# Loads of the next stage issued in the last turn of the stage before, and channel mixing's first keys taken chunk by chunk

## The reference

```python
# time mixing (RWKV): mixes, projections, a scan over the 128 rows, group norm, gate
x = x + att * g @ Wo.T
# channel mixing
xn2 = _ln(x, ln2_w, ln2_b)
sx2 = _token_shift(xn2, state[:, i0])     # row t-1 minus row t
xk = xn2 + sx2 * ffn_maa_k
xr = xn2 + sx2 * ffn_maa_r
rr = jax.nn.sigmoid(xr @ ffn_Wr.T)
kk = jnp.square(jax.nn.relu(xk @ ffn_Wk.T))
x = x + rr * (kk @ ffn_Wv.T)
# twice cross attention with 16 heads of 128 on keys and values of ctx, then an MLP 512 -> 2048 -> 512 with gelu
x = x + cross_attention(layer_norm(x), ctx, ...)
x = x + cross_attention(layer_norm(x), ctx, ...)
x = x + gelu(layer_norm(x) @ w_fc1 + b_fc1) @ w_fc2 + b_fc2
```

## Time and profile before

| | before |
|---|---|
| median of 3 runs | 3049.38 us (3048.84 to 3049.61) |
| the profiled execution, its own time | 3048.88 us |
| its span, first to last instruction | 3047.1 us |
| mean granted clock of TensorE | 0.975 of full speed |
| busy: PE, DVE, ACT, POOL | 94%, 58%, 38%, 18% |

### The profile page before, as it was taken

One profiled execution on the slowest core, in us unless ns is written; L12 is line 12 of the kernel. 1 busy time (PEld: TensorE's weight loads), 2 busy tenths in 40 slices (PEclk: granted clock), 3 DMA queues, 4 the chain that ended last, 5 costly groups with the idle time before them and its releaser, 6 DMA issues.

```text
span 3047.1 us, 40885 instructions
## 1 busy us (share of the span) xinstructions
PE 2878.6 (94%) x14864; PEld 2177.5 (71%) x14864; DVE 1776.0 (58%) x2615; ACT 1162.6 (38%) x2537; POOL 536.5 (18%) x375
## 2 busy tenths in 40 slices
PE   5989898985979999999999999999999999999899
PEld 2333333333768888888888878788888888888787
DVE  5989889895755444455444464454444554444644
ACT  3232323232434343445334343344334444433432
POOL 2857667571001000000000010010000000000100
PEclk8999899997999999999999999999999999999999
DMA  5010010102223111111111112121111111111011
GB/s 160 1 29 28 23 34 2 41 1 99 73 101 133 38 37 49 38 56 39 47 43 35 55 35 62 44 88 38 55 38 39 48 39 55 38 50 32 23 54 55
DMA packets 54780, 148.72 MB, mean 49 GB/s; under 512 B 6256, under 2 KB 7536, under 8 KB 53584
## 3 DMA queue, kind: packets, MB, share of 16 engines
q1 hardware_dynamic: 51824, 143.80, 14.2%
q0 software_dynamic: 2880, 3.94, 0.6%
HBM read 131.20 MB, written 12.58 MB: 47 GB/s over the span
## 4 chain that ended last, share of the span: by engine, by line
PE 67%; DVE 2%; ACT 1%; issue 0%; DMA 0%; ACTq 0%; DVEq 0%
PE ca_ps L60 19%; PE ca_ps L62 19%; PE ca_ps L61 19%; PE ca_ps L1967 4%; PE ca_ps L1951 4%; PE ca_ps L1959 2%; PE ca_ps L1993 1%; DVE ca_stats L68 0%; DVE ca_xres L1728 0%; DMA ca_xres<-in_ctxT 0%; DVE ca_wq_lo L1686 0%; ACT ca_sk L1644 0%; DVE ca_ctx_lo L1759 0%; DVE ca_h_lo L1753 0%; ACT L1644 0%
## 5 line engine op out<-in xcount | busy, mean ns | idle before, releaser
L1728 DVE TENSOR_TENSOR ca_xres<-ca_xres,ca_ps 128x512 f32<-128x512 f32 x384 | 263.9, 687 | 244.1 <-PE ca_ps L62 239.1
L1515 ACT ACTIVATE ca_pr<-ca_ps,ca_nb 128x129 f32<-128x129 f32 x512 | 181.4, 368 | 511.3 <-DVE ca_nb L1711 511.2
L60 PE MATMUL ca_ps<-ca_h_hi,ca_wq_hi 128*128 128x512 f32 x768 | 313.2, 408 | 3.8 <-DVE ca_h_lo L1753 3.3
L613 DVE TENSOR_TENSOR_SCAN tm_xn<-tm_wd,tm_vb 128x512 f32<-128x512 f32 x256 | 298.5, 1208 | 12.7
L62 PE MATMUL ca_ps<-ca_h_hi,ca_wq_lo 128*128 128x512 f32 x768 | 303.0, 394 | 0.0
L61 PE MATMUL ca_ps<-ca_h_lo,ca_wq_hi 128*128 128x512 f32 x768 | 301.0, 392 | 0.0
L60 PE MATMUL ca_ps<-ca_wv_hi,ca_ctx_hi 128*128 128x256 f32 x1024 | 297.9, 291 | 0.0
L62 PE MATMUL ca_ps<-ca_wv_hi,ca_ctx_lo 128*128 128x256 f32 x1024 | 287.4, 281 | 0.0
L61 PE MATMUL ca_ps<-ca_wv_lo,ca_ctx_hi 128*128 128x256 f32 x1024 | 287.2, 280 | 0.0
L1468 POOL TENSOR_TENSOR ca_dv<-ca_bvr 128x256 f32<-128x256 f32 x32 | 24.7, 772 | 1453.7 <-DVE ca_v L1696 1443.7
L60 PE MATMUL ca_ps<-ca_wo_hi,ca_ct_hi 128*128 128x512 f32 x640 | 253.5, 396 | 0.2 <-DVE ca_xres L1728 0.2
(11 more groups left out here) (232 smaller groups left out, 5788.4 us busy)
## 6 DMA issues: line engine op xcount, KB each, us to landing
ca_sq<-in_wq SPq DMA_DIRECT2D x49, 512.0 KB, 5.2
ca_so<-in_wo SPq DMA_DIRECT2D x48, 512.0 KB, 3.5
ca_sk<-in_wk SPq DMA_DIRECT2D x33, 512.0 KB, 6.4
ca_sv<-in_wv SPq DMA_DIRECT2D x32, 512.0 KB, 3.6
ca_bvr<-in_bvb SPq DMA_DIRECT2D x32, 256.0 KB, 3.9
tm_xq<-in_x SPq DMA_DIRECT2D x16, 256.0 KB, 3.8
tm_xres<-in_x SPq DMA_DIRECT2D x4, 1024.0 KB, 5.1
x_dram<-tm_xres SPq DMA_DIRECT2D x4, 1024.0 KB, 4.3
```

Source lines behind the costliest of these rows:

```text
L60: pe.matmul(out, lhs[0], rhs[0], start=first, stop=False)
L613: v.tensor_tensor_scan(state[t % 2][:, d, :], wd[:, g].rearrange("p b t -> p (b t)"), pair[:, d, :], 0.0, ALU.mult, ALU.add).then_inc(scan ...
L1515: ins = act.activation(pr[hd][:, b, :], ps[:, BANK_SC + b // 2, o:o + KW], ACT.Exp, bias=nbs[hd][:, b:b + 1], scale=SCALE, accum_out=sms[h ...
L1728: v.tensor_tensor(xres[U.h][:, U.quad * 4 + b, :], xres[U.h][:, U.quad * 4 + b, :], ps[:, BANK_O + b % 2, :], ALU.add).then_inc(o_out, 1)
```

## The change

Loads that a stage began with are issued by the preceding stage. `xq`, `xres`, `eps`, the constants and a tensor `raw` of 12 x 512 columns now belong to all stages; time mixing's weights `wv`, `wk`, `wr` are the three parts of `raw`, and so are channel mixing's `gate`, `relu`, `gy`. In the last turn of time mixing SP issues channel mixing's five first loads, each weight when its third of `raw` has been read for the last time, and then the last store. In the last turn of channel mixing it issues six loads of cross attention ahead of the last store. The wait for the last store moves from the end of a block into the next one: in channel mixing to the head of SP's stream, in cross attention behind the first load of `x3`. On DVE and PE channel mixing's first keys are written chunk by chunk. In `first()` ACT's `key_out(C, 0)` goes ahead of `roots(0)`.

```diff
 # time_mix, SP
+            def store(q):
+                sp.wait_ge(res_added, q * 4 + 4)
+                sp.dma_start(x2[bass.ds(q * 4, 4)].rearrange("b t e -> t b e"), xres[:]).then_inc(x2_out, 16)
...
-                sp.wait_ge(res_added, q * 4 + 4)
-                sp.dma_start(x2[bass.ds(q * 4, 4)].rearrange("b t e -> t b e"), xres[:]).then_inc(x2_out, 16)
-            sp.wait_ge(x2_out, NQ * 16 + 16)
+                    store(q)
+            sp.wait_ge(xn0_ready, NQ * 4)
+            sp.dma_start(xq[:], x2[0:4].rearrange("b t e -> t b e")).then_inc(cm_first_in, 16)
+            sp.dma_start(common["prev0"][:], io["prev0"]).then_inc(cm_first_in, 16)
+            for w, (full, count) in enumerate(((v_full, NQ * 4), (k_full, NQ * 4), (r_full, NQ * 4))):
+                sp.wait_ge(full, count)
+                sp.dma_start((wv, wk, wr)[w], io["l0w"][5 + w]).then_inc(cm_first_in, 16)
+            store(NQ - 1)
 # channel_mix, SP
-            sp.dma_start(xq[:], x2[0:4].rearrange("b t e -> t b e")).then_inc(x_in, 16)
-            for tile, name in ((vec, "vec"), (ident, "ident"), (prev, "prev0")):
-                sp.dma_start(tile[:], io[name]).then_inc(const_in, 16)
-            for j in range(3):
-                sp.dma_start(raw[j][:], io["l0w"][5 + j]).then_inc(w_in[j], 16)
+            sp.wait_ge(x2_out, NQ * 16 + 16)
...
                 sp.dma_start(xres[:], x2[bass.ds(q * 4, 4)].rearrange("b t e -> t b e")).then_inc(res_in, 16)
+                if not more:
+                    sp.dma_start(early["ctx"][:, 0:4, :], io["ctxT"][:, :, 0:QT]).then_inc(early["c_in"][0], 16)
+                    sp.dma_start(early["ctx"][:, 4:8, :], io["ctxT"][:, :, QT:2 * QT]).then_inc(early["c_in"][1], 16)
+                    sp.dma_start(early["sk"][:], io["wk"][0]).then_inc(early["wk_in"], 16)
+                    sp.dma_start(early["sv"][:], io["wv"][0]).then_inc(early["wv_in"], 16)
+                    sp.dma_start(early["hv"][:], io["head_vec"]).then_inc(early["const_in"], 16)
+                    sp.dma_start(early["bvr"][:], io["bvb"][0]).then_inc(early["dv_in"], 16)
                 sp.wait_ge(added, q * 4 + 4)
...
-            sp.wait_ge(x3_out, NQ * 16 + 16)
 # channel_mix, DVE
+            def first_mix():
+                v.tensor_copy(xn[:, :, :, 0], prev[:, :, 0:4]).then_inc(prev_ready, 1)
+                v.wait_ge(prev_ready, 1)
+                for c in range(EC + 1):
+                    if c < EC:
+                        v.wait_ge(xn_ready, c + 1)
+                        v.tensor_tensor(sx[:, c, :] ...
+                        v.wait_ge(sx_ready, c + 1)
+                        v.scalar_tensor_tensor(out=xf[0][:, c, :] ...
+                    if c > 0:
+                        v.wait_ge(hi_ready, c)
+                        v.tensor_tensor(x_lo[0][:, c - 1, :], xf[0][:, c - 1, :], x_hi[0][:, c - 1, :], ALU.subtract).then_inc(split_ready, 1)
 # channel_mix, PE
-            keys(0)
+            for c in range(EC):
+                pe.wait_ge(split_ready, c + 1)
+                for f in range(EC):
+                    ins = mm3(pe, mm[:, f, :], (w_hi[:, 0, c, f * P:(f + 1) * P], w_lo[:, 0, c, f * P:(f + 1) * P]),
+                              (x_hi[0][:, c, :], x_lo[0][:, c, :]), c == 0, c == EC - 1)
+                    if c == EC - 1:
+                        ins.then_inc(k_full, 1)
 # cross_attend, ACT, first()
-                act.wait_ge(const_in, 48)
-                act.wait_ge(ready, 1)
+                act.wait_ge(const_in, 16)
+                key_out(C, 0)
                 roots(0)
-                key_out(C, 0)
                 key_out(C, 1)
```

More of the change, by code:

```diff
@@ L103, in sem @@
             return ctx.enter_context(nc.semaphore("tm_" + n))
-        vec = sb("vec", [P, NV])
-        ident = sb("ident", [P, P])
+        vec, ident, eps, xq, xres, raw = [common[n] for n in ("vec", "ident", "eps", "xq", "xres", "raw")]
+        wv, wk, wr = [raw[:, j * EC:(j + 1) * EC, :] for j in range(3)]
         head_sum_u = sb("head_sum_u", [P, EC, P])
@@ L1007, in _, with channel_mix @@
             closing(NQ - 1)
-def channel_mix(nc, io, x2, x3):
+def channel_mix(nc, io, x2, x3, common, early):
     with ExitStack() as ctx:
@@ L1018, in sem @@
             return ctx.enter_context(nc.semaphore("cm_" + n))
[L1020 to L1023, removed]
+        vec, ident, eps, prev, xq, xres = [common[n] for n in ("vec", "ident", "eps", "prev0", "xq", "xres")]
+        gate, relu, gy = [common["raw"][:, j * EC:(j + 1) * EC, :] for j in range(3)]
         rest = sb("rest", [1, 1])
@@ L1152, in link, with norm @@
                 return step
-            def norm(q):
-                v.wait_ge(x_in, q * 16 + 16)
+            def norm(q, first=False):
+                if first:
+                    v.wait_ge(first_in, N_FIRST)
+                else:
+                    v.wait_ge(x_in, q * 16)
                 layernorm_dve(v, xq, lnx, stats, mv, std, rstd, bn_done, stats_ready, std_ready, xn0_ready, q, link(q))
@@ L1264, in _, with cross_attend @@
             values(NQ - 1)
-def cross_attend(nc, io, x3, out):
+def cross_attend(nc, io, x3, out, common, early):
     HT = 8
@@ L1291, in cross_attend @@
         h2 = two("h", [P, EC, HT * L])
-        xres = [sb("xres%d" % h, [P, HT, E]) for h in range(2)]
-        lt = sb("lt", [P, 4, E])
+        xres = [common["raw"][:, 0:HT, :], early["ctx"]]
+        lt = common["raw"][:, HT:HT + 4, :]
         stats = sb("stats", [P, 4, 6])
@@ L1461, in _ @@
         def _(gp):
-            gp.memset(eps[:], EPS).then_inc(ready, 1)
             def value_bias(i):
@@ L2110, in build, with sb, sem @@
     x2 = nc.dram_tensor("x2_dram", (B, L, E), F32, kind="Internal").ap()
-    time_mix(nc, io, x2)
     x3 = nc.dram_tensor("x3_dram", (B, L, E), F32, kind="Internal").ap()
-    channel_mix(nc, io, x2, x3)
-    cross_attend(nc, io, x3, out)
+    with ExitStack() as whole:
+        def sb(n, s, d=F32):
+            return whole.enter_context(nc.sbuf_tensor(n, s, d))
+        def sem(n):
+            return whole.enter_context(nc.semaphore(n))
+        common = {"vec": sb("vec", [P, NV]), "ident": sb("ident", [P, P]), "eps": sb("eps", [P, 1]),
+                  "prev0": sb("prev0", [P, EC, B]), "xq": sb("xq", [P, 4, E]), "xres": sb("xres", [P, 4, E]),
+                  "raw": sb("raw", [P, 3 * EC, E]), "cm_first_in": sem("cm_first_in"),
+                  "x2_out": sem("x2_out"), "x3_out": sem("x3_out")}
+        time_mix(nc, io, x2, common)
+        early = {"hv": sb("ca_hv", [P, 11 * NH]), "ctx": sb("ca_xres1", [P, 8, E]), "sk": sb("ca_sk", [P, EC, 256]),
+                 "sv": sb("ca_sv", [P, EC, 256]), "bvr": sb("ca_bvr", [P, 2, 256]),
+                 "c_in": [sem("c_in%d" % quad) for quad in range(2)],
+                 "wk_in": sem("wk_in"), "wv_in": sem("wv_in"), "dv_in": sem("dv_in"), "const_in": sem("const_in")}
+        channel_mix(nc, io, x2, x3, common, early)
+        cross_attend(nc, io, x3, out, common, early)
 def vec_table(a):
```

75 lines of the change are left out of this document (30 added, 45 removed).

## The result

| | before | changed |
|---|---|---|
| median | 3049.11 us of 4 runs (3048.76 to 3049.61) | 3026.31 us of 4 runs (3024.28 to 3033.33) |
| the profiled execution, its own time | 3048.88 us | 3033.33 us |
| its span | 3047.1 us | 3031.4 us |
| mean granted clock | 0.975 | 0.977 |

The ratio is 0.9927 (95% interval 0.9913 to 0.9941), 22.8 us by the medians; I had said 21.1 and 3028.3. Note that the profiled execution of the changed kernel is the slowest of its four, 7 us above the median. The explanation has to account for that too.

What follows compares the result with a forecast made beforehand. PE, busy 94% of the span, was taken as the bound, with its longest stalls at the two seams. Terms 3.9 + 8.0 − 0.9 + 3.9 + 5.8 + 0.4 = 21.1 us off gave 3028.3 us, range 3024.0 to 3033.0.

Steps and rivals of the forecast that it cites:

- Store waits, 3.9 + 3.9: End of time mixing and of channel mixing: moving the last store's wait behind the barrier takes 3.9 us off each.
- The rival that a block end holds the engines: Both block ends wait for outstanding DMAs anyway, so the 3.9 us stay: gain 13.3, time 3036; chance 0.07.
- First seam, 8.0: Time mixing to channel mixing: early loads bring the first `xn` 8.05 instead of 16.07 us after the barrier, 8.0 off.
- Chunked keys, 0.9 lost: Channel mixing's first turns: keys end 2.5 us earlier, but idle PE and a fallen clock make it net 0.9 lost.
- PE, being late, would wait less in the next turn: Channel mixing's second turn: PE, slowed in the values, waits less and may keep its clock, giving 1.0 us back.
- Rule on the clock: Second transposes of channel mixing: about 3.5 us of idle PE drops the clock, so they take 3.65 us, not 1.97.
- Second seam, 5.8: Channel mixing to cross attention: early loads start PE 5.62 instead of 11.46 us after the barrier, 5.8 off.
- `first()`, 0.4 gained: Cross attention's first unit: with `key_out(C, 0)` ahead of the roots, the first query comes 0.4 us earlier after PE's start.
- A second slip: Second seam: the forecast had the rows of `x3` land 5.8 us after their request, as `xq` did.
- The rest, no change: From cross attention's first query to the end, the time should be that of before.

Runs made afterwards that it cites:

- e2: Changed kernel with the waits for the last stores put back at the end of both blocks, loads still early: 3034.11 us, ratio 0.9947.
- e3: Changed kernel's tensor placing only; loads late, store waits at block ends, keys and roots order as before: 3053.77 us, ratio 1.0011 to the kernel before.
- e1: Changed kernel with channel mixing's first keys and first mix as before, without chunks: 3023.60 us, ratio 0.9913.
- e11: The changed kernel itself, unaltered, timed again in the last group: 3024.50 us, ratio 0.9924.
- e0: The changed kernel itself, unaltered, timed again in the second group: 3027.51 us, ratio 0.9936.
- e7: Changed kernel with the second half of ctx rounded and split earlier in `first()`: 3024.82 us, ratio 0.9921.
- e8: Changed kernel with the roots ahead of the first `key_out` again, as in the kernel before: 3025.47 us, ratio 0.9924.
- third profile: Trace of a later run of the unaltered changed kernel (`e11_changed_third`): span 3022.8 us.
- e5: Changed kernel, chunks kept; ACT rounds second and third weight after the first roots, DVE makes the third's low part after the first squares: 3023.19 us, ratio 0.9921.

## Why the prediction came out right, and where its terms were off

- **Store waits, 3.9 + 3.9.** Right: from the last store to the barrier's release it is 0.81 us in both places, 3.9 and 4.3 less than before. They stand behind the barriers now, and e2 shows that they cost 7.6 where they stood. The rival that a block end holds the engines is refuted by e2 against the changed kernel.
- **First seam, 8.0.** Right: barrier to N is 7.86 us in the profile after (728.66 to 736.52), 8.2 off. The transposes took 3.67 of the forecast 3.65. That the early loads did it is shown by e2 against before (store to N 8.3 us shorter with the wait still in place), and by e3, where they are late and the gain is gone.
- **Chunked keys, 0.9 lost.** The mechanism was right: keys at N + 4.5 (forecast 4.4), ACT's second weight at N + 8.31 (8.16), the second transposes at N + 31.88 (31.65 before, and 0.2), idle time 3.99 (3.5), fallen clock. Two things were off. The sum was: 0.2 + 1.4 (3.36 − 1.97 for the slow transposes), of which 1.8 came back where I had put 1.0, so the whole stretch is 0.15 shorter than before and not 0.9 longer. And the reason for what came back was wrong. I had said that PE, being late, would wait less in the next turn. But from the second transposes to the last store e1, without chunks, takes 118.87 us against before's 120.70: also 1.8 less. Before simply had its clock fall in its own second turn (2.99 us for the transposes) and e1 had not; no run shows that the edit is the cause. e3, which has the loads late and these keys as before, kept its clock there as well (1.96 us after a wait of 1.80) and took 150.58 from N to the last store. So the 0.15 rests on one trace of before, in which the clock fell. Set against the same kernel without them, the chunks cost 0.9 to 2.3 us, and the fall of the clock is an accident on top: with 2.89 us of idle time in e11 it held, with 3.99 it fell. The longer idle time came from a clock that had risen sooner in the keys (receptances at N + 16.85 against N + 17.93).
- **Rule on the clock.** The Trainium skill, TensorE: Matmul & The Clock Gate (Part 1), has an idle PE fall to 1.2 GHz. The rows agree at 3.99 us (0.50); after 2.89 us (e11) the granted clock was still 1.00, and the 16 transposes took 1.96. My forecast took it from a stall of 3.30 us and was right for the profiled execution only: in e0, e7, e8 and e11 the stall was 2.86 to 2.90 us and the clock held.
- **Second seam, 5.8.** Right: 11.46 to 5.54, so 5.9.
- **`first()`, 0.4 gained.** Wrong in sign: 0.28 lost. The chain started earlier as I had said (DVE's `wq_lo` 10.71 us after the first key, 11.05 before), but the two took 3.02 us and not 2.40, both times beside GpSimd's addition of the bias. That is 0.62 − 0.34. Why they took 3.02 and not 2.40 stays open, but what the new order is worth is told by e8, 0.24 gained. A second slip had no effect there: the rows of `x3` were used 7.45 us after the request, not 5.8. The roots do not notice it behind `key_out`; in e8, where they stand first, they do: the second key starts 7.34 us after the first, and before 6.64. The Trainium skill, ScalarE: Activation LUTs (What ACT_TABLE_LOAD costs), gives 2.66 us for a switch with its drain. The rows differ and decide: the load takes 1.28 us, the root starts 1.30 us behind its start (901.35, 902.65), and `key_out` ahead of it ends at 901.34.
- **The rest, no change.** Right for the third profile (−0.5 and −0.3), not for the first (+3.9 and +2.6), where the clock differs in unchanged code. I had no term for that, and the range of 3024.0 to 3033.0, made from other causes, happened to span it: single runs of the changed kernel went from 3023.8 to 3033.9. That the median came out within 2 us of the forecast is therefore in part luck; the terms of the two seams are not.

The sum of the edits is 22.2 us in the first profile (3.9 + 8.2 + 0.15 + 4.3 + 5.9 − 0.3) and 23.6 in the third, against 21.1 forecast. Most of what was missing is the 0.9 that the chunks did not cost against before, or more where the clock held. What stays open is what sets the clock in the stretches that no edit touches.

## What to carry to other kernels

The part of a stall at a stage boundary that is a load's flight or a store's landing goes away when the loads move into the stage before and the wait for the last store moves behind the barrier; what stays is the chain of first instructions (here 7.86 us to N and 5.54 us to the first key). Each term of the seams could be read off the old trace to within 0.4 us. An earlier start on an engine whose next wait is for another engine becomes mostly idle time there, and idle time can cost the clock: first look who releases that wait and give the time to that chain. e5 did so and took 1.5 us off the stretch of the changed kernel, of which the chunks themselves hold 0.35. Where the clock changes from execution to execution, compare stretches between named instructions in several traces, since a difference of 1 to 2 us is lost in the totals.
